# A decoder layer on one core: the light feed-forward's Gelus and second product leave the steps of the routing and run during search, choice and places

## The reference, cut to what matters

```python
def ffn(x, gamma, w1, b1, w2, b2):
    h = rms_norm(x, gamma)
    h = jax.nn.gelu(h @ w1 + b1, approximate=False)
    return h @ w2 + b2

def coor_descent_route(x, routing_token, num_tokens):
    s = jnp.einsum('bnd,d->bn', x, routing_token)
    constant = EPS * jnp.log(K_ROUTE)                 # EPS 0.1, K_ROUTE 8
    b0, a0 = -relu(s), 0
    def step(carry, _):                               # 50 times
        a_prev, b = carry
        a = constant - EPS * logsumexp((s + b) / EPS, axis=-1, keepdims=True)
        b = -relu(s + a)
        return ((a, b), None)
    ...
    scores = jnp.exp((s + a + b) / EPS)
    sel_scores, sel_idx = jax.lax.top_k(scores, num_tokens)    # 512 of 2048
    return (sel_scores + stop_gradient(1.0 - sel_scores), sel_idx)

light_out = ffn(x, gamma_light, w1_light, b1_light, ...)       # 512 -> 256 -> 512, all tokens
sel_scores, sel_idx = coor_descent_route(x, routing_token, 512)
routed_out = ffn(x[batch, sel_idx], gamma_heavy, ...)          # 512 -> 2048 -> 512
heavy_out = zeros_like(x).at[batch, sel_idx].set(routed_out * sel_scores[..., None])
x = x + light_out + heavy_out
```

## Time and profile before

| What | us |
|---|---|
| median of the three runs | 4175.44 |
| the profiled execution's own time | 4174.66 |
| its span, first to last instruction | 4172.9 |
| `routed`, from 3692.6 to the end of the span | 480.3 |
| of it: first transfer to the first light product (3717.06) | 24.5 |
| first light product to the spreading of the scores (3864.30) | 147.2 |
| spreading to the heavy layer's first product (3936.65) | 72.4 |
| from there to the end of the span | 236.3 |

### The profile page before, as it was taken

One profiled execution on the slowest core, in us unless ns is written; L12 is line 12 of the kernel. 1 busy time (PEld: TensorE's weight loads), 2 busy tenths in 40 slices (PEclk: granted clock), 3 DMA queues, 4 the chain that ended last, 5 costly groups with the idle time before them and its releaser, 6 DMA issues. The chain is left out here.

```text
span 4172.9 us, 59357 instructions
## 1 busy us (share of the span) xinstructions
PE 3949.2 (95%) x18740; PEld 2163.9 (52%) x18740; DVE 2413.5 (58%) x3306; ACT 2064.6 (49%) x3413; POOL 2704.0 (65%) x1413
## 2 busy tenths in 40 slices
PE   7979999999999999999999999999859999957799
PEld 6754444444444444444444444444348888844344
DVE  3346666666666666666666666666227777734400
ACT  2225555555555555555555555555425555527110
POOL 1008888888888888888888888888824444310100
PEclk9979999999999999999999999999879999979999
DMA  6633222322223332322232222322033333365300
GB/s 188 166 85 81 60 58 56 95 67 61 56 83 79 95 102 58 99 61 60 56 89 73 61 56 75 86 59 54 16 114 97 106 101 103 92 218 167 106 10 10
DMA packets 393922, 350.50 MB, mean 84 GB/s; under 512 B 193131, under 2 KB 267371, under 8 KB 392808
## 3 DMA queue, kind: packets, MB, share of 16 engines
q1 hardware_dynamic: 325864, 326.28, 27.1%
q10 hardware_dynamic: 66048, 16.78, 1.8%
q0 software_dynamic: 1920, 6.29, 0.5%
HBM read 142.88 MB, written 89.70 MB: 56 GB/s over the span
## 5 line engine op out<-in xcount | busy, mean ns | idle before, releaser
L254 POOL TENSOR_TENSOR acc<-acc,probs 128x1024 f32<-128x1024 f32 x896 | 2131.9, 2379 | 268.9 <-ACT probs L664 142.2
L771 DVE TENSOR_REDUCE maxes<-ps 128x1 f32<-128x1024 f32 x1024 | 1250.1, 1221 | 672.5 <-PE ps L482 667.9
L667 ACT ACTIVATE probs<-ps,far_bias 128x1024 f32<-128x1024 f32 (+7 forms) x1280 | 1022.1, 820 | 1019.2 <-DVE near_s L788 558.5
L517 PE MATMUL ps<-probs,v_head 128*64 128x512 f32 x4096 | 997.1, 608 | 5.4 <-ACT ctx_out L650 5.3
L482 PE MATMUL ps<-stacks 64*128 64x512 f32 x2048 | 752.4, 448 | 13.6 <-DVE maxes L771 11.0
L497 PE MATMUL ps<-stacks 64*128 64x512 f32 x1792 | 661.9, 449 | 0.0
L496 PE MATMUL ps<-stacks 128*128 128x512 f32 x2048 | 619.2, 419 | 0.0
L497 PEld LDWEIGHTS ps<-stacks 64*128 64x128 f32 x1792 | 277.0, 185 | 504.9 <-issue 340.4
L517 PEld LDWEIGHTS ps<-probs,v_head 128*64 128x64 f32 x4096 | 249.3, 136 | 488.8 <-issue 482.4
L496 PEld LDWEIGHTS ps<-stacks 128*128 128x128 f32 x2048 | 351.3, 189 | 216.1 <-issue 164.4
L788 DVE TENSOR_TENSOR near_s<-ps,near_bias 128x384 f32<-128x384 f32 (+2 forms) x576 | 284.4, 494 | 287.2 <-PE ps L497 262.5
(11 more groups left out here) (236 smaller groups left out, 4912.2 us busy)
## 6 DMA issues: line engine op xcount, KB each, us to landing
stacks<-c_k SPq DMA_DIRECT2D x128, 256.0 KB, 2.4
stacks<-c_q SPq DMA_DIRECT2D x128, 256.0 KB, 2.6
stacks<-c_d SPq DMA_DIRECT2D x256, 128.0 KB, 2.6
scr_v<-c_k ACTq DMA_DIRECT2D x32, 512.0 KB, 4.0
stacks<-c_q SPq DMA_DIRECT2D x128, 128.0 KB, 2.5
v_head<-scr_v SPq DMA_DIRECT2D x32, 512.0 KB, 3.7
sums<-scr_inv SPq DMA_DIRECT2D x128, 128.0 KB, 2.9
scr_ctx<-ctx_out SPq DMA_DIRECT2D x128, 128.0 KB, 2.3
```

Source lines behind the costliest of these rows:

```text
L254: pool.tensor_tensor(acc[:, qb, :], acc[:, qb, :], pr, ALU.add).then_inc(s["summed"], 1)
L517: mm = pe.matmul(ps[64 * half:64 * half + 64, PV, :], v_head[:, side, kt, :], probs[:, st % PT_RING, half * 512:(half + 1) * 512], start=k ...
L667: ins = act.activation(probs[:, st % PT_RING, a:z], sc[:, a:z], ACT.Exp, bias=bias)
L771: dve.tensor_reduce(maxes[:, qt, pair:pair + 1], ps[:, bank:bank + 2, :], AX.XY, ALU.max).then_inc(s["max_done"], 1)
```

## The change

In `routed` alone:

- A step carries 4 matrix products of the light layer's first product instead of 8, from step 2 on, so all 48 remaining steps have them. Gelus and second products have left the steps.
- ScalarE runs the 16 Gelus after it has copied the spread scores. Of the 32 light tiles 20 run in the 5 levels (four each), one behind each of the three matrix groups of the choice, five between the one-hot products of the first batch, four behind that batch's places.
- The one-hot products are in float32r: `what` has four columns (the token number and the weight, each in two parts that are exact or summed later) instead of two, and VectorE adds the parts (`parts4`). Half of the second batch's one-hot products stand between the heavy layer's first products.
- The maximum over partitions is taken by a transpose and a product on TensorE instead of on GpSimd; the light weights are scaled and split by ScalarE (in step 0) and VectorE (in step 1).
- `w1` is scaled by ScalarE in 16 pieces of 128x512, one behind the logarithm of each of steps 33 to 48, instead of by VectorE behind the places.
- SP issues the light layer's second weights after the first two chunks, the residuals behind chunk 2, and the heavy weights and the constants behind chunk 3.

```diff
-HIDDEN_FROM, HIDDEN_STEP = 3, 8
+HIDDEN_FROM, HIDDEN_STEP = 2, 4
...
+LIGHT_IN_LEVEL = 4
+def light_of_level(lv):
+    return list(range(LIGHT_IN_LEVEL * lv, LIGHT_IN_LEVEL * (lv + 1)))
+LIGHT_IN_STEP = LIGHT_IN_LEVEL * LEVELS
+LIGHT_AT_PLACE = {t: LIGHT_IN_STEP + 3 + i for i, t in enumerate(range(2, NT, 3))}
+LIGHT_LAST = list(range(LIGHT_IN_STEP + 3 + len(LIGHT_AT_PLACE), NTILES))
+GAMMA_PIECES = HEAVY // 512
+GAMMA_FROM = 33
...
+        hot = sb("hot", [P, 2, NUM_HEAVY], F32R)
+        what = sb("what", [P, NB, NT, 4], F32R)
... SP
             for ch in range(2, NCHUNK):
                 sp.wait_ge(s["hidden_mm"], LM * (ch - 1))
                 tokens_in(ch)
+                if ch == 2:
+                    for j in range(4):
+                        xb_in(j)
+                if ch == 3:
+                    for dst, name in LOADS:
+                        sp.dma_start(dst[:], io[name]).then_inc(s["weights"], 16)
... TensorE
                 for ch, m, at in hidden_of(i):
                     hidden_mm(ch, m, at)
-                for j in light_of(i):
-                    light_mm(j)
...
-                if LIGHT_IN_LOOP + lv < NTILES:
-                    light_mm(LIGHT_IN_LOOP + lv)
+                for j in light_of_level(lv):
+                    light_mm(j)
...
+            for t in range(NT):
+                hot_mm(0, t)
+                if t in LIGHT_AT_PLACE:
+                    light_mm(LIGHT_AT_PLACE[t])
+            pairs_turned(0)
+            for j in LIGHT_LAST:
+                light_mm(j)
+            for t in range(NT - HM // 2):
+                hot_mm(1, t)
... ScalarE
-                if i == GELU_AFTER:
-                    ...
+                if i == 0:
+                    act.wait_ge(s["wl1_in"], N_HIDDEN)
+                    for k in range(KT):
+                        ins = act.activation(wl1_hi[:, k, :], wl1[:, k, :], ACT.Identity, scale=gamma_l[:, k:k + 1])
+                    ins.then_inc(s["wl1_hi"], 1)
+                piece = i - GAMMA_FROM
+                if 0 <= piece < KT * GAMMA_PIECES:
+                    ...
+                    act.activation(part, part, ACT.Identity, scale=gamma[:, k:k + 1]).then_inc(s["gam"], 1)
...
             act.copy(rows[:], ps[:, 4:8, :].rearrange("p a n -> p (a n)")).then_inc(s["bcr"], 1)
+            act.wait_ge(s["light_in"], N_LIGHT)
+            for q in range(NCHUNK * LM):
+                part = hidden[:, q % LM, q // LM * TOKENS:(q // LM + 1) * TOKENS]
+                act.wait_ge(s["hidden"], q + 1)
+                act.activation(part, part, ACT.Gelu, bias=bl1[:, q % LM:q % LM + 1]).then_inc(s["gelu_l"], 1)
... VectorE
-                if lv and LIGHT_IN_LOOP + lv - 1 < NTILES:
-                    light_out(LIGHT_IN_LOOP + lv - 1)
+                if lv:
+                    for j in light_of_level(lv - 1):
+                        light_out(j)
...
+                    if b == 0 and t - 1 in LIGHT_AT_PLACE:
+                        light_out(LIGHT_AT_PLACE[t - 1])
...
+                if b == 0:
+                    for j in LIGHT_LAST:
+                        light_out(j)
-            for k in range(KT):
-                ins = dve.tensor_scalar(w1[:, k, :], w1[:, k, :], gamma[:, k:k + 1], None, ALU.mult)
-            ins.then_inc(s["gam"], 1)
```

## The result

The changed kernel takes 4122.84 us (median of 4 runs, 4117.52 to 4132.32) against 4173.95 for the kernel before on the same chip (4 runs, 4164.42 to 4177.79). The ratio is 0.9885, with a 95% interval of 0.9869 to 0.9901: 1.1% faster. The profiled execution of the changed kernel is the slowest of its four, 4132.32 us with a span of 4130.5. Its routing begins 3694.56 us into the span and takes 435.9 us instead of 480.3. In a later comparison one of 17 runs of the kernel before took 7495.76 us, and it is left out of every ratio and median here.

A forecast was written before the change was run, and what follows sets the result against it. The routing's chain of waits bounds the kernel: GpSimd's start, TensorE's light products, ScalarE's table loads, then search and places. 47.65 + 0.7 = 48.4 us won from 4174.66 gives 4126.3, plus 1.7 makes 4128; range 4114 to 4154.

The forecast's parts named there:

- The likeliest case: Whole routing: the change works as summed, 4128 us, 1.1% faster; chance 0.74.
- Steps: Routing's 48 remaining steps: 1.85 us each at full clock, 88.8 us, against 3.06 us for a step with loads.
- a piece of `w1`: Scaling behind each logarithm on ScalarE: 16 x 0.05, say 0.8 us in all; at worst 11.3.
- Half clock in the steps: Rival: TensorE pauses each step and runs at half clock, 2.4 us instead of 1.85, so 4151 us; chance 0.12.
- Loads: ScalarE's table loads in the steps: reckoned at the measured 1.283 us each, not the skill page's about 2.7 us.
- Search: After the scores' spreading: four light tiles and a flag make a level 7.25 us, five levels, paced by TensorE.
- Tiles paced by transfers: Rival: light tiles limited to about 215 GB/s take 2.4 us instead of 1.73, so 4148 us; chance 0.08.
- One-hot groups: First batch's places: three one-hot products with a light tile between groups take 3.7 us; heavy layer starts at 3889.0.
- The first chunk: Routing's start: tokens issued about 3694.6 land 8.1 us later, at 3702.7, a bound on light products starting at 3704.3.
- Chunk 4: Step 26: tokens queued behind 4 MB of w1 cause a wait of 0 to 4.3 us, taken as 2.7.
- what was added for hand-overs: Whole sum: 1.7 us added to 4126.3 for hand-overs left out, giving 4128 us.

The follow-up runs named there:

- the two experiments with loads: Kernel before with one combined exponential-logarithm table set loaded after the Gelus: 4151.88 us; changed kernel with a tiny Gelu in step 26, bringing loads back: 4164.01 us.
- With the loads back: Changed kernel plus a 128x16 Gelu on a spare tile in step 26, so table loads return from step 27 on: 4164.01 us, ratio 0.9987.
- the second profile: Changed kernel run again unchanged, in a later comparison on one chip: 4118.06 us, ratio 0.9876, routing 434.3 us.

## Why the prediction was right

The forecast was 4128 us, and the median came out at 4122.84. The likeliest case held, step by step:

- **Steps.** Forecast 1.85 us, measured 1.84, in steps with a piece of `w1` as well (0.8 us were set aside for these; they cost nothing). That the loads go is the largest part, and the two experiments with loads show it from both sides.
- **Half clock in the steps** did not come, but for the few steps behind chunk 4: 1.00 from 3714.50 to 3753 and again after 3767. The rule on brief idling between groups of matmuls (the Trainium skill, "TensorE: Matmul & The Clock Gate", section "A second HAM failure mode: psum-queue depth-cycling") does not decide here; a pause of 0.4 us in every step left the clock at its upper level, 2.4 GHz. With the loads back the half clock did come with brief idling: that kernel's clock fell in the wait for chunk 4, was 1.00 again from 3751 to 3753, and fell to 0.50 behind the next pause, where it stayed to the end of the steps. The pauses of the kernel before, 0.85 us a step beside its light tiles, had left it at 1.00. TensorE's next pause with the loads back:

```profile
3754.23 0.58 PE L1610 MATMUL r_ps<-r_ex,r_ones 128*128 128x32 f32 x2 [1.63 <-ACT r_ex L1714]
```

- **Loads.** All loads seen took 1.283 us. The 2.7 us that the prediction set beside them is a price for a whole change of tables: the Trainium skill, "ScalarE: Activation LUTs", section "What ACT_TABLE_LOAD costs", has about 1283 ns for the load and about 1380 ns for a drain. The load agrees; a drain does not show, as the function starts 0.01 us behind its load (3775.89 and 1.28, then 3777.18, in the step shown above).
- **Search.** 38.4 us against 39.2, the first level slow at a clock of 0.81, the other four set by TensorE.
- **Tiles paced by transfers** did not come: 1.74 us a tile at 290 GB/s, 1.73 at 312.
- **One-hot groups** 3.69 us against 3.7, and the heavy layer begins 35.2 us after the first tile against 35.0.

The sum was too small in two terms, both waits for tokens. The first chunk was bounded by 8.1 us to landing; it took 10.93 and its products began 2.0 us later than forecast (0.4 in the second profile). The 8.1 is the median of all 16 parts. Of the first chunk's two parts in the kernel before, the second took 9.4 us, and it is issued 0.6 us behind the first, so the trace at hand had the better figure. Chunk 4 was priced at 2.7 us of 0 to 4.3. TensorE's timeline has the measured wait, and SyncE's has why:

```profile
3708.22 0.80 PE L1593 MATMUL r_ps<-r_t,r_wl_hi 128*128 128x512 f32 x1 [1.82 <-DMA r_t<-scr_t]
...
3759.06 0.80 PE L1593 MATMUL r_ps<-r_t,r_wl_hi 128*128 128x512 f32 x1 [5.31 <-DMA r_t<-scr_t]
```

```profile
3730.85 1.50 SPq L1522 DMA_DIRECT2D r_t<-scr_t  x2
3732.40 0.61 SPq L1541 DMA_DIRECT2D r_w<-in_w1h  x1
...
3741.90 6.16 SPq L1522 DMA_DIRECT2D r_t<-scr_t  x2
```

Chunk 4 landed 28.2 us after chunk 3's issue (3730.85 to 3759.06) where 26.5 was reckoned. The wait of 5.31 us also took the clock to 0.50 for the steps behind it, which was not in the sum. The stage is 7.1 us longer than the one with `w1` in pieces. Together these terms and the smaller ones put the routing 4.0 us above the sum in the first profile and 2.4 in the second. Of this 1.7 was covered by what was added for hand-overs, and that was luck: it was meant for something else.

Three slips in the prediction change no sum. The search was said to take 19.2 us more than now; by its own marks it is 39.2 against 19.2, so 20.0 more. The reading that TensorE set the pace in the steps ahead of the Gelus leaves out the 6.7 us that it waited for chunks there. And in the stretch that gave the 1.85 TensorE did not wait for the chain, it was busy throughout (columns of the earlier trace rows):

```profile
3726.74:3728.59 1.85, 1.85 (x10) 1.35 (x9) 0.78 (x5) 0.44 (x3) 0.00 (x0) 1.00 0.77 200
```

The 1.85 held all the same: in that step the sum followed its exponential after 0.06 us (3726.97 to 3727.03), about as in the changed kernel.

That the median nevertheless lies 5 us below the forecast is not the routing's doing. The forecast assumed the start of the routing as in the first profile of the kernel before (3692.59); the changed kernel has started it at 3694.56 and at 3681.20. The routing accounts for 44.4 us (first profiles) to 48.6 us (482.9 less 434.3); the medians differ by 51.1 us here and by 53.7 in the later comparison on one chip (4171.77, the median of 16 runs, less 4118.06). Whether the rest is spread or belongs to the version is not settled.

## What to carry to other kernels

Count the table loads in a chain of small steps before anything else: where one set holds both alternating functions, as here, loading it by name once takes the loads away, and the work that the loads happened to cover must find another place before the whole gain is seen. Put the moved work where the engine that does it waits for another one's chain (one tile a level kept within VectorE's pace here, 19.1 us for five levels; with four they took 38.4), and look at what a large transfer that is moved forward stands in front of in its queue: cut into pieces between the urgent ones, it held none of them up here. Take a transfer's time to landing from the place in the program where it will run, not from the median of all of them.

## What the hardware showed that was not expected

- One wait of 5.31 us was enough for the granted clock to fall to 0.50 behind it, while 0.4 us of pause in every step left it at 1.00. A shorter wait had the same effect in the kernel before, for a chunk of tokens between full steps at 1.00 (TensorE's timeline, then a stretch in the columns of the earlier trace rows):

```profile
3733.94 0.50 PE L1586 MATMUL r_ps<-r_t,r_wl_hi 128*128 128x512 f32 x1 [2.36 <-DMA r_t<-scr_t]
```

```profile
3735.50:3737.00 1.50, 1.50 (x5) 1.22 (x4) 0.00 (x0) 0.00 (x0) 0.00 (x0) 0.50 1.05 393
```

- A float32 one-hot product costs more than its own records: the eight heavy records behind it took 3.63 us instead of 3.43.
- The same program's unchanged first part differed by 13.4 us between two executions, nearly all of it outside the long loop over the heads.
